# Attention followed by a block-sparse feed-forward layer: the first steps of the sparse layer are placed at other units of the attention

## The reference

```python
x = x + L0_xattn(layernorm(x), ctx, ctx, Wq, Wk, Wv, Wo)
x = x + L0_ffn(layernorm(x), c1_w, c2_w, w1, w2t)
...
def L0_xattn(query, key, value, Wq, Wk, Wv, Wo):   # 32 heads of 16, 8 key heads
    q, k, v = heads(query @ Wq), heads(key @ Wk), heads(value @ Wv)
    probs = softmax(q @ k.T * 16 ** -0.5)
    return merge(probs @ v) @ Wo

def L0_ffn(x, c1_w, c2_w, w1, w2t):                # INTER 1792, RANK 16, SPARSITY 32
    inter = x @ c1_w.T @ c2_w.T                    # cheap scores of 1792 hidden units
    idx = argmax(inter.reshape(-1, 56, 32), -1) + arange(0, 1792, 32)
    h = relu(einsum('bkm,bm->bk', w1[idx], x))     # one winner in each block of 32
    return einsum('bk,bkm->bm', h, w2t[idx])
```

## Time and profile before

| | before |
|---|---|
| median of 3 runs | 1539.59 us (1537.06 to 1543.56) |
| profiled execution, its own time | 1538.27 us |
| span in the profile | 1536.5 us |
| mean granted TensorE clock | 0.967 of full speed |
| busy in the span: PE, DVE, ACT, POOL | 91%, 70%, 50%, 47% |
| the attention's exponentials run from | 23.9 to about 160 us |
| first hidden tile of the sparse layer on PE | 179.4 us |
| end of the two layers | about 372 us |

### The profile page before, as it was taken

One profiled execution on the slowest core, in us unless ns is written; L12 is line 12 of the kernel. 1 busy time (PEld: TensorE's weight loads), 2 busy tenths in 40 slices (PEclk: granted clock), 3 DMA queues, 4 the chain that ended last, 5 costly groups with the idle time before them and its releaser, 6 DMA issues. The chain is left out here.

```text
span 1536.5 us, 31522 instructions
## 1 busy us (share of the span) xinstructions
PE 1399.7 (91%) x11353; PEld 835.5 (54%) x11368; DVE 1079.3 (70%) x2119; ACT 768.9 (50%) x2486; POOL 720.6 (47%) x748
## 2 busy tenths in 40 slices
PE   5779779897999999987999999999999688889998
PEld 4667334344777777634655555555555235434444
DVE  7988455553666775766988888888877788966212
ACT  4777454121433343345766666666665356745111
POOL 4788343001443443763766666666665405734000
PEclk9999789999999999998999999999999898989999
DMA  7999742113899989865865645556544501645000
GB/s 183 195 155 161 154 102 64 31 32 86 164 171 176 201 149 142 143 138 126 172 136 103 145 107 112 135 115 112 107 77 80 136 0 22 137 83 106 16 18 28
DMA packets 520410, 173.58 MB, mean 113 GB/s; under 512 B 478416, under 2 KB 503440, under 8 KB 520256
## 3 DMA queue, kind: packets, MB, share of 16 engines
q1 hardware_dynamic: 520256, 171.57, 57.3%
HBM read 53.27 MB, written 2.10 MB: 36 GB/s over the span
## 5 line engine op out<-in xcount | busy, mean ns | idle before, releaser
L1960 POOL TENSOR_TENSOR a_q_ss<-a_q_ss,half 128x4 f32<-128x4 f32 x64 | 90.2, 1409 | 167.1 <-DVE a_k_ss L1869 83.7
L1782 ACT ACTIVATE a_probs<-a_masked,a_negmax 128x128 f32<-128x128 f32 x256 | 100.0, 392 | 100.8 <-DVE a_negmax L1840 100.8
L68 PE MATMUL bank<-a_wq_hi,xn_pair 128*128 128x512 f16 (+1 forms) x384 | 141.0, 367 | 8.9 <-DVE a_kn L1874 5.1
L1299 POOL TENSOR_TENSOR a_p_hl<-a_probs,a_p_hl 128x512 f16<-128x512 f32 x64 | 74.4, 1163 | 141.6 <-DVE a_p_hl L1223 141.6
L69 PE MATMUL bank<-a_wq_lo,xn_pair 128*128 128x512 f16 (+1 forms) x384 | 140.7, 366 | 0.0
L70 PE MATMUL bank<-a_wq_hi,xn_pair 128*128 128x512 f16 (+1 forms) x384 | 140.5, 366 | 0.0
L68 PE MATMUL bank<-a_wo_hi,a_o_hi 128*128 128x512 f16 x256 | 97.5, 381 | 4.4 <-DVE x_state L1856 3.5
L69 PE MATMUL bank<-a_wo_lo,a_o_hi 128*128 128x512 f16 x256 | 97.5, 381 | 0.0
L70 PE MATMUL bank<-a_wo_hi,a_o_lo 128*128 128x512 f16 x256 | 97.3, 380 | 0.0
L1975 POOL TENSOR_TENSOR a_normal<-a_probs,a_recip 128x512 f32<-128x512 f32 x64 | 90.6, 1415 | 5.0
L688 POOL TENSOR_TENSOR a_p_hl<-a_probs,a_p_hl 128x512 f16<-128x512 f32 x64 | 78.8, 1241 | 21.3 <-DVE a_p_hl L609 14.7
(11 more groups left out here) (466 smaller groups left out, 5043.7 us busy)
## 6 DMA issues: line engine op xcount, KB each, us to landing
a_no<-in_L_xattn_Wo SPq DMA_DIRECT2D x9, 1024.0 KB, 5.8
a_nq<-in_L_xattn_Wq SPq DMA_DIRECT2D x8, 1024.0 KB, 5.8
f_n<-in_L_ffn_w SPq DMA_DIRECT2D x6, 512.0 KB, 4.1
f_n<-in_L_ffn_w2t SPq DMA_DIRECT2D x6, 512.0 KB, 3.9
a_n_wq<-in_L_xattn_Wq SPq DMA_DIRECT2D x4, 768.0 KB, 5.1
a_n_wo<-in_L_xattn_Wo SPq DMA_DIRECT2D x4, 768.0 KB, 5.5
a_nk<-in_L_xattn_Wk SPq DMA_DIRECT2D x9, 256.0 KB, 3.1
a_nv<-in_L_xattn_Wv SPq DMA_DIRECT2D x9, 256.0 KB, 3.1
```

The lines of the kernel that those rows point to most:

```text
L68: pe.matmul(out, lh, rh, start=start, stop=False)
L1299: pool.tensor_tensor(p_hl[s % PN][:, 1, t, :], probs[unit(s, t) % PROBS][:, :, :].rearrange("p h n -> p (h n)"), p_hl[s % PN][:, 0, t, :], ...
L1782: m = act.activation(probs[s % 2][:, h, :], src, ACT.Exp, bias=negmax[s % 2][:, h:h + 1], accum_out=total[s % 2][:, h:h + 1])
L1960: pool.tensor_tensor(r[:, :], r[:, :], K.half[:, 0:n], ALU.pow).then_inc(root_done.sem, 1)
```

## The change

It moves work of the sparse layer between steps, and some of it between engines; nothing is added to what is computed.

- **Rows.** The first four rows are normalised on DVE in one piece at step 64 (`normalise_early`), no longer on ACT at 57 to 63; `shift` and its two small POOL instructions go. The turns are at steps 64, 64, 65, 65 and no longer 64 to 67.
- **Small factors.** Loaded at step 50 (before 8), cleared by POOL at 51 (8), high halves on ACT at 53 and 57 (20, 22, 24). Their low halves go from POOL at 30 to DVE at 65, directly from the unscaled factors, so ACT's scaling pass (L2441) goes.
- **w1's first piece** comes in one transfer at step -1 into a place of its own, `landing`, is scaled by ACT at 45 (32) and finished by POOL at 66 (32). The pieces w1 1, w2 0 and w2 1 are loaded at 66 (68, the w2 piece 0 at 28 and 36).
- **POOL's other work.** `CONSTANTS` from 40 to 67, clearing `cx_s` from 49 to 65, the roots from 54 to 57.
- **Pieces beside the hidden tiles.** `SPLIT` in steps of the sparse layer: w1 of q at 2q - 3 (before 2q - 4), w2 of q at 2q (before 2q - 3, w2 0 at -1).
- **Second half.** Rows of batches 4 to 7 at steps 6 to 9 (7 to 10), their first picks at 9 to 12 (11, 12, 13, 13).

```diff
-    FIRST, LAG, RING, MASKS = -BESIDE + 8, 4, 2, 4
-    before_start = lambda t: t - BESIDE
-    LOAD_SMALL, LOAD_FIRST, LOAD_SECOND = before_start(8), [before_start(t) for t in (12, 16, 20, 24, 28, 36)], -3
-    CLEAR_SMALL, SMALL_HIGH, SMALL_LOW, CONSTANTS, CLEAR = (before_start(t) for t in (8, 20, 30, 40, 49))
-    MEANS, LATER = before_start(54), 6
-    AHEAD_ROWS = {0: -14, 1: -12, 2: -10, 3: -8}
-    TURN = {0: -7, 1: -6, 2: -5, 3: -4}
-    ROWS = {4: 7, 5: 8, 6: 9, 7: 10}
-    PICK = {(b, i): (4 * i - 5 if i else -4) + b if b < HALF else 4 * (i + 1) + b if i else min(7 + b, NT - 1)
+    FIRST, LAG, RING, MASKS = -BESIDE - 2, 4, 2, 4
+    beside = lambda t: t - BESIDE
+    LOAD_FIRST, LOAD_SMALL, LOAD_SECOND = beside(-1), beside(50), beside(66)
+    CLEAR_SMALL, SMALL_HIGH, SMALL_LOW = beside(51), (beside(53), beside(57)), beside(65)
+    MEANS, ROOTS, CLEAR, CONSTANTS, LATER = beside(56), beside(57), beside(65), beside(67), 5
+    NORMAL, FIRST_LOW = beside(64), beside(66)
+    TURN = {0: beside(64), 1: beside(64), 2: beside(65), 3: beside(65)}
+    ROWS = {4: 6, 5: 7, 6: 8, 7: 9}
+    PICK = {(b, i): (4 * i - 5 if i else beside(67)) + b if b < HALF else (4 * (i + 1) if i else 5) + b for b in range(B) for i in range(PARTS)}
...
-    SPLIT = {("w1", 0): before_start(32), ("w1", 1): -2, ("w2", 0): -1, ("w2", 1): 0}
-    SPLIT.update({(kind, q): 2 * q - 4 + i for q in range(2, PIECES) for i, kind in enumerate(("w1", "w2"))})
+    SPLIT = {("w1", 0): beside(45), ("w1", 1): -2, ("w2", 0): 0, ("w2", 1): 2}
+    SPLIT.update({("w1", q): 2 * q - 3 for q in range(2, PIECES)})
+    SPLIT.update({("w2", q): 2 * q for q in range(2, PIECES)})
...
+    landing = nc.alloc_sbuf_tensor_at(f"{N}_landing", piece_of["w1"], F32, offset=landing_at)
...
-            for i in [i for i, when in enumerate(LOAD_FIRST) if when == t]:
-                load_first(i)
+            if t == LOAD_FIRST:
+                sp.dma_start(landing[:, :, :], w1.rearrange("(k p) f -> p k f", p=P)[:, :, 0:2 * P]).then_inc(first_in, 16)
             if t == LOAD_SECOND:
                 over.queries_made(sp)
                 load(("w1", 1))
+                load(("w2", 0))
                 load(("w2", 1))
...
+        def normalise_early(b):
+            if b == 0:
+                dve.wait_ge(root_done, 2)
+                over.rows_used(dve)
+            dve.tensor_scalar(xn[b][:, :], K.x[:, b, :], mv[:, b, 0:1], rstd[:, b:b + 1],
+                              ALU.subtract, ALU.mult).then_inc(normal_done.sem, 1)
+
+        def low_of_small(i):
+            if i == 0:
+                dve.wait_ge(small_hi.sem, 2)
+            for kind in (("c1", "c2"), ("c2",))[i]:
+                dst, src = small(kind)
+                if kind == "c1":
+                    dve.scalar_tensor_tensor(dst[1], src, WS, dst[0], ALU.mult, ALU.subtract).then_inc(small_lo.sem, 1)
+                else:
+                    cols = (slice(0, SPAN * P), slice(SPAN * P, HID))[i]
+                    dve.scalar_tensor_tensor(dst[1][:, cols], src[:, cols], WS, dst[0][:, cols],
+                                             ALU.mult, ALU.subtract).then_inc(small_lo.sem, 1)
...
-            for b in at(TURN, t):
+            if t == NORMAL:
+                for b in early:
+                    normalise_early(b)
+            if t == SMALL_LOW:
+                low_of_small(0)
+            for b in at(TURN, t - 1):
                 low_of_row(b)
+            if t == SMALL_LOW:
+                low_of_small(1)
```

78 lines of the change are left out of this document (29 added, 49 removed).

## The result

The changed kernel takes 1526.41 us (median of four runs, 1525.15 to 1528.15); the kernel before, run beside it, 1540.48 us. The ratio is 0.991 with a 95% interval from 0.9886 to 0.9934, that is 10 to 18 us less; the medians lie 14.1 us apart. The forecast was 11.8 us less, 1527.8 us.

What follows compares the result with a forecast made beforehand. The prediction took DVE and POOL together to pace the units, and small-step chains with waits to follow. Its terms, -6 + 1 - 1.5 - 1.9 - 3.4 = -11.8 us, from 1539.6 gave 1527.8 us, range 1518 to 1537.

Steps and rivals of the forecast that it cites:

- units and start: Units: work shed by POOL and ACT gives -6 us (-12 to 0); early w1 transfer delays turned probabilities, +1 (0 to +3).
- tail: Behind the last unit: normalisations fit DVE's idle time, row halves no longer delay products; -1.5 us, range -2.4 to +3.
- first hidden tiles: Two of ACT's four weight passes between hidden tiles 0 and 1 go: -1.9 us, at most -2.4.
- second half: Picks at steps 9 to 12 remove the mask wait and slow matmuls, add a ring stall: -3.4 us, range -5.7 to 0.
- half the price: Units: the batch with c2's low half shows 2 us for POOL's 3.9, so 12 us of shed work gives 6.
- DVE's own stream as the pace: Rival, chance 0.20: DVE's own work paces the units, which then give 0; total -5.8 us, 1533.8 us.
- One resource with the price in full: Rival, chance 0.20: DVE and POOL act as one in the units, all 12 us come off; -17.8, 1521.8 us.
- the casts' median nearer to 0.41 us: Sign of being right: in the units, the casts of L609 get a median nearer to 0.41 us (0.768 before).
- Gain 2 x 1.2, loss 0.9: -1.5: Behind the last unit: two product halves on DVE each come 1.2 us sooner; factors' low halves delay by up to 0.9.
- The rival in which the tail becomes DVE's: Chance 0.07: DVE's added work and POOL's burst put +8.7 us before the first rank-16 product, units give 0; +4.4, 1544.0 us.
- The wait that I named: PE's wait of 2.44 us at 197.19 us, for the hidden tile behind ACT's four passes; upper limit of that gain.
- A third step with one ring use too many: Second half: the earlier picks add a third ring stall to the two there, at 1.13 us each; +1.1 us.

Runs made afterwards that it cites:

- experiment 11: Changed kernel with the small factors wholly as before: loaded and cleared at 8, high halves at 20, 22, 24, low halves on POOL at 30; 1525.93 us.
- experiment 5: Changed kernel with the weight pieces beside the hidden tiles back at their old steps, transfers as changed; 1529.45 us.
- 4: Changed kernel with the rows and first picks of batches 4 to 7 back at their old steps; 1529.65 us.
- experiment 12: Kernel of experiment 11 with w1's first piece, its ACT passes and POOL's low half, also back at unit 32; 1524.92 us.
- experiment 2: Changed kernel with POOL's low half of the first w1 piece at unit 46 and the constants at unit 40; 1527.65 us.
- experiment 6: Changed kernel with the 512 KB transfer of the first w1 piece at unit 20, not ahead of unit 0; 1530.16 us.
- experiment 8: Changed kernel with four rank-16 products in one step, picks two a step, the rest of c2's low half behind the products' halves; 1520.83 us.
- Experiments 7: Changed kernel with the first four rows normalised on ACT at units 57, 59, 61, 63 again, shifts on POOL; 1526.16 us.
- 3: Changed kernel with the second part of c2's low half (1280 columns on DVE) four steps later; 1526.89 us.
- experiment 1: Changed kernel with the small factors' loading, clearing and ACT high halves back at 8, 8, 20, 24, low halves still on DVE; 1525.48 us.

## Why the prediction was right, term by term

| term | forecast | by position | by experiment |
|---|---|---|---|
| units and start | -6 and +1 | -8.2 | see below |
| tail | -1.5 | +2.8 | -4.1 without DVE's low halves (11) |
| first hidden tiles | -1.9 | -3.0, of which -1.6 one slow stretch | -2.8 (5), of which -1.7 one slow stretch |
| second half | -3.4 | -4.7 | -4.7 behind tile 5 (4) |
| sum | -11.8 | -13.1 | |

The total was right with one term of the wrong sign, made up by the three others: the tail came out 4.3 us worse than forecast, units and start 3.2 us better, the hidden tiles 2.4. That the sum lies within 2.3 us of the medians' difference is luck in that part.

**Units: mechanism right, size of its parts off.** "So it shows some 2 us for POOL's 3.9, half the price": it was 3.2 for 3.91 (experiment 11; the same instruction took 3.58 before). It held a DVE instruction to its end in each of the three kernels that have it: the key mask in the kernel before and in experiment 12, a cast in experiment 11. (The mask of the earlier trace rows began inside POOL's instruction and ended 0.5 us behind it; the prediction had it lie inside.) The other end is as true: 4.1 us of POOL's work in five instructions cost 1.1, at most 1.8 (experiment 2). A mean price of half came near only because both kinds were in it. What I costed at nothing was not nothing: the clearing cost 1.5 to 2 us at whichever unit it stood, and ACT's high halves with it 3.4 in units 48 to 55. Of the rivals, DVE's own stream as the pace is refuted: c2's low half, w1's piece and the clearing all showed. One resource with the price in full comes near for c2's low half and the clearing, not for the rest. Of the signs named, the casts' median nearer to 0.41 us did not come (0.776).

**Start.** "+1" was 0: exponentials begin at 23.7 us (23.9 before), and the first eight units are the same with and without the early transfer (experiment 6).

**Tail: the step that failed** is "Gain 2 x 1.2, loss 0.9: -1.5". Of the gain 0.4 us came. The first 1.2 was to come at the half of the first product, ahead of the first score; there DVE's own new work stands in front of it, and it is part of the loss. The second came as forecast (a wait of 1.76 us is 0.53), but the clock was already down at the first score product, and 0.8 of it went into slower matmuls; in experiment 2, where the clock falls 2.1 us behind that product (before the change 1.8), the same order takes 10.6 us from there to the first hidden tile, not 11.8. What the prediction did not see is that the chain's own order, one product and one score in turn, is the same before and after; experiment 8, which breaks it, wins 6.0 us behind the first score product. The loss was 3.1 us and not 0.9 (first score product 11.60 us behind the last exponential, before 8.46): normalisations of 3.81 us for 2.1, low halves of the factors of 4.25 for 2.7, and all of it ahead of the first product's half. Experiments 7, 3 and 11 take parts of this work away and bring that score 1.4, 2.1 and 2.5 us sooner (11 against experiment 1). The rival in which the tail becomes DVE's had this mechanism right; its price of 8.7 was too high, since the rows start with POOL's burst and not behind it, and its other half, units without a gain, did not come.

**First hidden tiles.** The wait that I named shrank by 1.6 us, and 1.4 of the 3.0 us can be put down to the pieces' new places. Experiment 5 gives back 1.1, though at another wait than mine. The rest is a stretch of 3.4 us at 1.2 GHz, which the kernel before and experiment 5 have at different places, which two kernels with the new places have too, and which the prediction did not hold. So the size of 1.9 lies between 1.1 and 3.0, and it is not shown that the cause was right for more than the smaller one.

**Second half.** The mask's wait went with the slow matmuls behind it, as forecast. "A third step with one ring use too many" did not come: two waits of 1.23 us stand at 238.8 and 246.7 where two of 1.13 stood before. That is 1.1 of the 1.3 us by which the term was too small.

## What to carry to other kernels

Price a move of work off POOL by what DVE does at that moment, instruction by instruction: one long instruction met by a cast cost four fifths of its length or more, the same time in shorter pieces elsewhere a quarter to under a half. When work is put into an idle stretch ahead of a chain of small steps, look first at the chain's own order: here regrouping four products and their picks took 6.0 of 11.4 us off that chain, more than any work that was moved in or out of the tail. And before a difference between two traces is put down to an edit, compare the granted clock behind each wait: in four of the kernels here one slow stretch was worth 1.4 to 1.7 us. And where a stretch has no slack, moving a pass "to another unit" is an edit with a price, which one group of units beside another shows.
